# Making z of a chunk's first tile one chunk ahead in a two-directional Mamba scan

## The reference, cut to what matters

```python
def _mamba(x, win, wconv, bconv, wx, wdt, bdt, Alog, Dp, wout):
    xz = x @ win.T
    u, z = jnp.split(xz, 2, axis=-1)                  # 1024 channels each
    u = jax.nn.silu(causal_conv(u, wconv) + bconv)    # 4 taps
    dbc = u @ wx.T                                    # dt (32), B (16), C (16)
    delta = jax.nn.softplus(dt @ wdt.T + bdt)
    dA = jnp.exp(delta[..., None] * -jnp.exp(Alog))
    dBu = (delta * u)[..., None] * Bm[:, :, None, :]
    h = dA_t * h + dBu_t                              # a scan over 4096 steps, 16 states
    y = (h * C).sum(states) + u * Dp
    y = y * jax.nn.silu(z)
    return y @ wout.T
```

## Time and profile before

| | us |
|---|---|
| median of the timed runs | 7401.91 |
| the profiled execution, its time | 7406.93 |
| its span | 7405.0 |

### The profile page before, as it was taken

The page is one execution under the profiler, slowest core; times in us unless marked ns, Lnnn a source line. Parts: engine busy times, 40 slices in busy tenths (PEclk is TensorE's granted clock), DMA queues, the critical chain, the costliest instruction groups (busy, mean ns, idle before and its releaser), DMA issues. The chain is left out here.

```text
span 7405.0 us, 108355 instructions
## 1 busy us (share of the span) xinstructions
PE 6731.3 (91%) x32416; PEld 4032.0 (54%) x32416; DVE 6877.8 (93%) x9234; ACT 6119.9 (83%) x13078; POOL 6953.7 (94%) x3764
## 2 busy tenths in 40 slices
PE   8999999999999999989999898999999999998799
PEld 5555555555555555555555555555555555555455
DVE  7999999999999999999999999999999999999766
ACT  6888888888888888888888888888888888888545
POOL 6999999999999999999999999999999999999678
PEclk9999999999999999999999999999999999999899
DMA  5455444445444444544444455344445544443155
GB/s 172 127 156 156 111 145 146 135 129 159 135 123 141 134 135 127 152 135 117 141 138 131 126 153 144 106 145 137 135 127 146 152 105 144 136 127 108 51 180 171
DMA packets 565933, 1006.64 MB, mean 136 GB/s; under 512 B 96624, under 2 KB 208368, under 8 KB 557552
## 3 DMA queue, kind: packets, MB, share of 16 engines
q1 hardware_dynamic: 559616, 993.54, 45.7%
q10 hardware_dynamic: 5744, 6.29, 0.3%
HBM read 875.49 MB, written 124.11 MB: 135 GB/s over the span
## 5 line engine op out<-in xcount | busy, mean ns | idle before, releaser
L517 POOL TENSOR_TENSOR dBu<-Bb,du 128x1024 f32<-128x1024 f32 x2048 | 4793.0, 2363 | 6.2 <-DMA Bb<-bc_scratch 4.7
L656 ACT ACTIVATE scans<-delta,A 128x512 f32<-128x512 f32 x4096 | 2745.0, 696 | 238.0 <-DVE hC L1160 216.6
L1144 DVE TENSOR_TENSOR_SCAN scans<-scans,state,dBu 128x512 f32<-128x512 f32 x2016 | 2533.4, 1277 | 228.5 <-ACT scans L656 224.0
L1144 DVE TENSOR_TENSOR_SCAN dBu<-scans,state,dBu 128x512 f32<-128x512 f32 x1568 | 1955.0, 1258 | 5.2 <-ACT scans L656 5.2
L892 PE MATMUL yT<-ident,hC 128*128 128x128 f32 x9216 | 1403.6, 283 | 289.0 <-DVE hC L1160 287.4
L1160 DVE TENSOR_TENSOR hC<-scans,Cb 128x512 f32<-128x512 f32 x2304 | 1551.0, 677 | 8.0 <-PE yT L892 7.8
L529 POOL TENSOR_TENSOR hR<-dBu,Cb 128x512 f32<-128x512 f32 x1024 | 1304.5, 1274 | 222.0 <-DVE dBu L1144 221.5
L892 PEld LDWEIGHTS yT<-ident,hC 128*128 128x128 f32 x9216 | 1087.2, 145 | 581.0 <-DVE hC L1160 364.6
L603 ACT ACTIVATE turned<-bg,CT 128x128 f32<-128x128 f32 x3072 | 875.0, 370 | 246.1 <-PE bg L869 245.7
L885 PE MATMUL bg<-u,comb 128*128 128x512 f32 x2048 | 963.6, 597 | 50.8 <-ACT pre L616 49.9
L843 PE MATMUL bg<-hT,win_z 128*128 128x512 f32 x2048 | 977.8, 600 | 0.0
(11 more groups left out here) (147 smaller groups left out, 7899.5 us busy)
## 6 DMA issues: line engine op xcount, KB each, us to landing
comb<-pre_scratch SPq DMA_DIRECT2D x992, 256.0 KB, 4.6
Bb<-bc_scratch SPq DMA_DIRECT2D x256, 512.0 KB, 6.9
Cb<-bc_scratch SPq DMA_DIRECT2D x256, 512.0 KB, 7.1
win_u<-in_win SPq DMA_DIRECT2D x256, 256.0 KB, 4.7
win_z<-in_win SPq DMA_DIRECT2D x256, 256.0 KB, 2.7
pre_scratch<-pre SPq DMA_DIRECT2D x248, 256.0 KB, 3.7
comb<-comb_scratch SPq DMA_DIRECT2D x61, 1024.0 KB, 7.2
part_scratch<-pre SPq DMA_DIRECT2D x128, 256.0 KB, 2.0
```

The lines of the kernel that those rows point to most:

```text
L517: pool.tensor_tensor(dBu[:, ring(g, q)], Bb[:, 2 * q:2 * q + 2, :], du[:, j % 2, :].unsqueeze(1).broadcast_to([P, 2, T]), ALU.mult).then_i ...
L656: act.activation(place(n)[:], delta[:, j % 2, :], ACT.Exp, scale=A[:, i // CH_DIR, j * N + n:j * N + n + 1]).then_inc(dA_made, 1)
L1144: nc.vector.tensor_tensor_scan(to, place(n)[:], dBu[:, ring(g, q), k, :], state[:, c:c + 1] if i % CH_SEQ else 0.0, ALU.mult, ALU.add).the ...
```

## The change

z of tile 0 is made in the chunk before, at positions 59 and 60, and taken at 62; its silu joins that of tile 7 in the visit at 63, so the visit at 7 is gone. z gets two places, one for even and one for odd tiles. Z7 moves from 58, 59 to 52, 53 and from bank 0 to bank 1; K, H0, H1, H2 move by up to two positions and change banks; the late comb product moves from 52 to 55. hR becomes a ring of three places, used in turn; to this end `wgain` goes to C's memory, and in the prologue the C loads from the fifth pair on wait for the gains' product. Z0 of chunk 0 is made in the prologue.

```diff
-HC, HR = 4, NA
+HC, HR = 4, 3
...
-    ("D1", (0,), 0), ("Z0", (1, 2), 1), ("O0", (2, 2, 3, 3, 4, 4, 5, 5), 0), ("O1", (6, 6, 7, 7, 9, 9, 10, 10), 0),
+    ("D1", (0,), 0), ("O0", (2, 2, 3, 3, 4, 4, 5, 5), 0), ("O1", (6, 6, 7, 7, 9, 9, 10, 10), 0),
...
-    ("X", (50, 51, 53, 54), 0), ("K", (56,), 1), ("D0", (56,), 0), ("Z7", (58, 59), 0), ("H0", (58,), 1),
-    ("H1", (60,), 1), ("H2", (61,), 0), ("H3", (62,), 1),
+    ("X", (50, 51, 53, 54), 0), ("Z7", (52, 53), 1), ("D0", (56,), 0), ("K", (58,), 0), ("Z0", (59, 60), 1),
+    ("H0", (60,), 0), ("H1", (61,), 0), ("H2", (62,), 0), ("H3", (62,), 1),
...
-GATED = {7: (("Z", 0),), 15: (("Z", 1),), 23: (("Z", 2),), 31: (("C", 0), ("Z", 3)), 39: (("C", 2), ("Z", 4)),
-         47: (("C", 4), ("Z", 5)), 53: (("C", 6), ("Z", 6)), 63: (("Z", 7),)}
+GATED = {15: (("Z", 1),), 23: (("Z", 2),), 31: (("C", 0), ("Z", 3)), 39: (("C", 2), ("Z", 4)),
+         47: (("C", 4), ("Z", 5)), 53: (("C", 6), ("Z", 6)), 63: (("Z", 7), ("Z", 0))}
...
-PROLOGUE = ([f"H{k}" for k in range(KD)] + [f"U{m}" for m in range(MT)] + ["X", "D0", "K"] + [f"H{k}'" for k in range(KD)] + ["G"])
+PROLOGUE = ([f"H{k}" for k in range(KD)] + [f"U{m}" for m in range(MT)] + ["Z0", "X", "D0", "K"] + [f"H{k}'" for k in range(KD)] + ["G"])
...
-COMB_AT, COMB_LATE = [3 + 2 * m for m in range(MT)], 52
+COMB_AT, COMB_LATE = [3 + 2 * m for m in range(MT)], 55
...
-        z = sb("z", [P, T])
+        z = sb("z", [P, 2, T])
...
-        wgain = hR
+        wgain = Cb[:, 8:12]
...
+                    if last is None and q == 4:
+                        sp.wait_ge(bg_ready, PRO)
...
-                                k = ASIDE.index(n)
+                                k = aside(g, n) % HR
...
-            def take_z(made, bank, g):
+            def take_z(made, bank, tile):
                 act.wait_ge(bg_ready, made)
-                act.wait_ge(gated, g + 1)
-                act.copy(z[:], bank[:]).then_inc(bg_free, 1)
+                act.wait_ge(gated, max(tile, 1))
+                act.copy(z[:, tile % 2, :], bank[:]).then_inc(bg_free, 1)
...
-            def silu_z(taken):
+            def silu_z(taken, k):
                 act.wait_ge(bg_free, taken)
-                act.activation(z[:], z[:], ACT.Silu).then_inc(z_made, 1)
+                act.activation(z[:, k % 2, :], z[:, k % 2, :], ACT.Silu).then_inc(z_made, 1)
```

More of the change, by code:

```diff
@@ L95 @@
 NUM_ACT = {name: e for e, name in enumerate(BY_ACT)}
-GATED = {7: (("Z", 0),), 15: (("Z", 1),), 23: (("Z", 2),), 31: (("C", 0), ("Z", 3)), 39: (("C", 2), ("Z", 4)),
-         47: (("C", 4), ("Z", 5)), 53: (("C", 6), ("Z", 6)), 63: (("Z", 7),)}
-assert all(TAKE[f"{kind}{m + (kind == 'C')}"] < p + (kind == "Z") and (kind == "C" or p // NQ == m) for p in GATED for kind, m in GATED[p])
+GATED = {15: (("Z", 1),), 23: (("Z", 2),), 31: (("C", 0), ("Z", 3)), 39: (("C", 2), ("Z", 4)),
+         47: (("C", 4), ("Z", 5)), 53: (("C", 6), ("Z", 6)), 63: (("Z", 7), ("Z", 0))}
+assert all(TAKE[f"{kind}{m + (kind == 'C')}"] < p + (kind == "Z") and (kind == "C" or p // NQ == (m if m > 0 else MT - 1)) for p in GATED for kind, m in GATED[p])
 assert sorted(m for p in GATED for kind, m in GATED[p] if kind == "C") == list(range(0, MT, 2))
 assert sorted(m for p in GATED for kind, m in GATED[p] if kind == "Z") == list(range(MT))
-PROLOGUE = ([f"H{k}" for k in range(KD)] + [f"U{m}" for m in range(MT)] + ["X", "D0", "K"] + [f"H{k}'" for k in range(KD)] + ["G"])
+PROLOGUE = ([f"H{k}" for k in range(KD)] + [f"U{m}" for m in range(MT)] + ["Z0", "X", "D0", "K"] + [f"H{k}'" for k in range(KD)] + ["G"])
 PRO = len(PROLOGUE)
@@ L114, in made_in @@
     if i == CHUNKS - 1:
-        return name[0] not in "UCXKH" and name != "D0"
+        return name[0] not in "UCXKH" and name not in ("D0", "Z0")
     return i < CHUNKS - 2 or name[0] != "H"
@@ L127 @@
 STATS_AT, RSTD_AT, NB_AT = (24, 32, 32, 40), 44, 48
-COMB_AT, COMB_LATE = [3 + 2 * m for m in range(MT)], 52
+COMB_AT, COMB_LATE = [3 + 2 * m for m in range(MT)], 55
 HALF_D = D // 2
-assert COMB_AT[-1] + 1 < AT["U1"][0] and AT["Z6"][-1] < COMB_LATE < AT["K"][0]
+assert COMB_AT[-1] + 1 < AT["U1"][0] and AT["Z7"][-1] < COMB_LATE < AT["Z0"][0]
 def batch_of_chunk(c):
@@ L427, in _ @@
                 load_wu(0, m)
+            sp.wait_ge(skip_stored, 32)
+            load_z(0, 0)
             sp.wait_ge(hist_made, MT + 1)
             store_hist(1)
-            sp.wait_ge(skip_stored, 32)
             sp.wait_ge(wtaps_stored, 32)
-            load_z(0, 0)
             sp.wait_ge(bg_free, PRO_NUM["X"] + 1)
@@ L691, in take @@
                 if kind == "Z":
-                    take_z(made, bank, g)
+                    take_z(made, bank, i * MT + (k if k > 0 else MT))
             nc.scalar.preload_act_table_set(SILU)
@@ L735, in _ @@
                     act.dma_start(wout, io["wout"][0].rearrange("(k p) n -> p k n", p=P)).then_inc(wout_loaded, 16)
+            take_z(PRO_NUM["Z0"] + 1, bg[PRO_NUM["Z0"] % 3], 0)
+            silu_z(PRO_NUM["Z0"] + 1, 0)
             nc.scalar.preload_act_table_set(EXP_LN)
@@ L775, in _ @@
                                     silu_u(freed(i, f"C{k + 1}"), k, 2, 1 - s)
-                                if kind == "Z":
-                                    silu_z(freed(i, f"Z{k}"))
+                                if kind == "Z" and made_in(i, f"Z{k}"):
+                                    silu_z(freed(i, f"Z{k}"), k)
                             nc.scalar.preload_act_table_set(EXP_LN)
@@ L785, in _ @@
                         if 1 <= i <= MT and p == COMB_LATE + 3:
[L786 removed]
+                            take_comb(MT + i - 1, bg[BANK["Z7"]])
                         if p == RSTD_AT and i + 2 < CHUNKS:
@@ L801, in bank_free @@
                     pe.wait_ge(comb_taken, MT)
-                elif 1 <= i <= MT and name == "K":
+                elif 1 <= i <= MT and name == "Z0":
                     pe.wait_ge(comb_taken, MT + i)
@@ L946, in background @@
                         if kind == "Z":
-                            project_z(bank, k, s, i * 64 + (k // 2) * 16 + 16, part(KD))
+                            project_z(bank, k, s if k > 0 else 1 - s, (i if k > 0 else i + 1) * 64 + (k // 2) * 16 + 16,
+                                      part(KD))
                         if kind == "X":
@@ L981, in _ @@
                     project_u(bank, 0, k, 0, range(KD))
+                if name == "Z0":
+                    project_z(bank, 0, 0, 16, range(KD))
                 if name == "X":
@@ L1014, in _ @@
                         if 1 <= i <= MT and j * NQ + q == COMB_LATE:
-                            pe.wait_ge(bg_free, freed(i, "Z6"))
-                            project_comb_late(bg[BANK["Z6"]], i - 1)
+                            pe.wait_ge(bg_free, freed(i, "Z7"))
+                            project_comb_late(bg[BANK["Z7"]], i - 1)
                         if q == 0:
```

6 lines of the change are left out of this document (2 added, 4 removed).

## The result

The changed kernel takes 7474.94 us (median of 4 runs), the kernel before 7400.05: a ratio of 1.0101, 95% interval 1.0083 to 1.0118, so 75 us slower. Timed once more later, it gave 7459.85 and 1.0088 [1.0072, 1.0104]. The forecast was 7446, and slower. The profiled execution's span is 7474.0 us against 7405.0.

A forecast was written before the change was run, and what follows sets the result against it. GpSimd bounds the kernel and, where it waits, VectorE; a chunk sums VectorE's path in two parts. Part A +15 and part B +29 give +44 us: 7446 us against the 7401.9 median; own range 7418 to 7475, 8 in 10 7388 to 7480.

The forecast's parts named there:

- Part B: VectorE's path from tile 3 to position 60: z of tile 7 at 52, 53 delays position 55; +29 us.
- Part A, the boundary: Chunk's end: second silu, second evacuation and z copy on ScalarE delay VectorE's next chunk; mean loss 1.3 us a chunk.
- Part A, tiles 0 and 1: Relief cut off at position 6, position 16 fixed 52.0 us behind position 0; with the boundary +15 us.
- rival 1: Faster: relief in tile 0 carries on, boundary loss 0, part of tile 1's wait gone; 7370 us, chance 0.18.
- The ring of three at nothing: Tile 2: GpSimd's fourth product waits 0.7 us for TensorE, hidden by its 1.34 us VectorE wait a tile later.
- Rival 3: The wait for TensorE in tile 2 is not covered, on top of the forecast: +19 us, 7465 us; chance 0.07.
- The prologue at nothing: Prologue: z of tile 0 falls into TensorE's wait for silu, its silu precedes a table load with spare time; no cost.

The follow-up runs named there:

- A later z of tile 7: Changed kernel with z of tile 7 at 55 and 56 and the late comb product back at 52: 7432.87 us, ratio 1.0037 to the kernel before.
- the shorter silu: Changed kernel with silu of z of tile 0 at 63 covering 32 of 512 columns: 7445.43 us, ratio 1.0059 to the kernel before.
- the ring of three alone: Kernel before with three places for products by C instead of four, `wgain` moved and later C loads: 7398.36 us, ratio 0.9991.
- paired silus: Kernel before with two places for z and silus of two tiles sharing a visit; four kernels: 7439.24, 7426.0, 7339.35 and 7356.87 us.

## Why the prediction was right, and where it fell short

- **Part B (z of tile 7 at 52, 53), 29 us: right.** Measured: 53 to 62 +0.93 us a chunk, 28 us, and position 54 in chunks 9 to 30 1.02 us longer (1.1 forecast), in chunks 1 to 8 0.6 (0.4 forecast). A later z of tile 7 takes all of it away in chunks 9 to 30. Which chunk loses how much was not forecast rightly (chunk 22: 0.9 us, not 1.94): TensorE's lead over VectorE changes from chunk to chunk and from one execution to the next. With the same lead the loss is the forecast one (1.98 us).
- **Part A, the boundary, 1.3 us a chunk: right.** +1.35. ScalarE's queue sets it, as the shorter silu shows. It includes what the forecast didn't name, some 0.15 us a chunk: in 3 chunks (4 in the other execution) 63 lasted 6.4 us, and in each of them the granted clock had fallen while VectorE was at position 60, where TensorE's H0 stands. In the two kernels with z of tile 7 at 55 and 56 there is no such fall and no 63 of 6.4 us. No run takes the fall away alone.
- **Part A, tiles 0 and 1: right.** Position 16 lies 52.0 us behind position 0 in 24 of 30 chunks, mean 52.00, and the waits of 2.75 us and 1.40 us at 14 and 16 are still there. The relief ends in TensorE's waits for VectorE at positions 1 and 4, and the products of position 6 are added no earlier (21.12 us behind position 0, 21.11 before), as forecast; rival 1 fell with this.
- **The ring of three at nothing: right**, and its cover was the one named. Rival 3 fell.
- **The clock at 15 to 17: missed, 18 us.** The prediction took the granted clock as a property of the boundary and let everything from 16 to 53 stand. TensorE's idle time of 1.61 us at 15 was there before, with a fall in 4 chunks of 31; with z a chunk ahead it falls in 12 to 18 of 31. That the idle time is a condition of the falls is shown by filling it; why they are more frequent is not known. The page TensorE: Matmul & The Clock Gate of the Trainium skill, section A second HAM failure mode: psum-queue depth-cycling, tells of a bf16 kernel whose short idle spells between groups of matmuls make the clock swing between its two levels. The trace of this fp32 kernel agrees in so far as the clock falls behind a short idle spell, in some chunks (0.66 against 1.00 behind the same 1.61 us).
- **The prologue at nothing: wrong, 2 to 4.5 us.** The first scan comes at 78.4 us, against 73.9 before and 73.2 and 73.3 in the two kernels without z in the prologue; with it, it was 76.1 to 78.4. Those two kernels have the later C loads as well, so it is z in the prologue that costs, and "falls into its wait for silu" was the step that failed.
- **Sum.** 44 forecast; +18 for the clock, +4.5 for the prologue, +2 for the boundary and tiles 0 and 1 (17 in chunks 1 to 30, for 15), -1 for part B (28 for 29), +3 at positions 23 to 52, +2 in chunks 0 and 31, -3.5 behind the last scan: 69.0 us. The miss against the median (75 us, 62 when timed again) is mainly the clock. The median of 7475 us lies at the upper end of the forecast's own range, 7418 to 7475, and inside it only with terms that weren't in the sum; the second timing lies well within. That range doesn't follow from its terms either: -4 to 30 and 10 to 40 give 7408 to 7472.
- **The table loads.** By the page ScalarE: Activation LUTs of the Trainium skill, section What ACT_TABLE_LOAD costs, a switch costs 2.66 us with its drain. The trace does not agree: in the changed kernel silu starts 1.30 us behind the load's start, and the next evacuation 1.30 us behind the start of the load back.

## What to carry to other kernels

Freeing an engine helps only up to the next point where it waits for another; read how far that is before counting the work taken away. Work moved into a slot lands on whatever transpose or evacuation stands behind it, and a load moved in an in-order DMA queue takes its wait along, ahead of everything issued later. An idle time that is harmless in one schedule can cost more in another through the granted clock, so look at the clock behind every gap and not only at its length. The same second place for z that cost 1% when it moved one visit gave 0.86% when every visit for z served two tiles and TensorE kept its schedule.

## What the runs showed of the hardware

TensorE's granted clock falls or stays behind the same idle time of 1.61 to 1.63 us, with the same distances, to some 0.01 us, between its rows of the 29 us ahead: in 1 of 31 chunks with z of tile 0 at positions 1 and 2 and z of tile 7 at 52, in 4 before, in 8 with the ring of three alone, in 12 to 18 with z a chunk ahead. With 1.56 us of matmuls whose result nobody reads in that gap it fell in none, and in none without the gap (paired silus). What decides between the kernels that leave the gap open is not settled by these runs.
